# Polynomial attention in a six-layer perceiver: order of the turns on TensorE, and of two low halves on GpSimd

## The chip, the cores and the metric

The kernel runs on one core of one Trainium2 chip. The metric is the device time of one execution in microseconds. The times below are of three runs of the kernel before, and one further execution was profiled.

## The reference, cut to what matters

Six layers follow one another on x (32 sequences of 32 tokens, 512 wide): a cross attention, an attention, a low-rank mixture, a second cross attention, the polynomial attention, and a mixture of experts. The change touches the fifth layer only, which the kernel runs in one stage together with the end of the fourth layer (its output projection) and the beginning of the sixth (layer norm and router logits):

```python
q1, k1 = (proj(Wq1), proj(Wk1)); q2, k2 = (proj(Wq2), proj(Wk2)); v = proj(Wv)
q1, k1 = (_apply_rotary(q1, cos, sin), _apply_rotary(k1, cos, sin))
q2, k2 = (_apply_rotary(q2, cos, sin), _apply_rotary(k2, cos, sin))
s1 = jnp.einsum('bqhd,bkhd->bhqk', q1, k1)
s2 = jnp.einsum('bqhd,bkhd->bhqk', q2, k2)
pattern = jnp.where(causal[None, None], s1 / D * (s2 / D), 0.0)
y = jnp.einsum('bhqk,bkhd->bqhd', pattern, v).reshape(B, T, C)
return y @ Wout.T
```

## The kernel before

Every float32 operand of a product is held as two float16 halves, a high and a low one, and `product` (L102 to L108) issues three matmuls for each: high by high, high by low, low by high. ScalarE makes the high half of a value, and VectorE or GpSimd the low half (the value less its high half).

The stage is `poly` (L1894). Its 1024 tokens are eight tiles of 128 rows. The stage runs in eleven slots s = 0 to 10, and each slot works on up to four tiles, one in each step of a pipeline: t = s (output projection of the layer before, residual, norm), b = s - 1 (the four projections with their rotations and the values), q = s - 2 (scores, patterns, attention product) and r = s - 3 (output projection of the attention, residual, second norm, router logits). The order of the work within a slot is written out by hand, once for each engine, in the loops over SLOTS at L2001 (GpSimd), L2107 (VectorE), L2199 (ScalarE) and L2314 (TensorE). Engines wait for one another by semaphores with constant counts.

Terms of the change, with their functions:

- A turn (`turn`, L2251) is four 128x128 transposes on TensorE into the one bank `pl_bT`. Each turn first waits until the low half of the turn before has been taken out of that bank. `turn_mat(m, b)` turns the rotated matrix m of tile b, after which ScalarE (`mat_high`, L2171) and VectorE (`mat_low`, L2075) take the halves. `turn_norm("a", t, ya)` turns the normed rows of tile t, and `turned_high` (L2167) and `turned_low` (L2071) take the halves into `pl_LT`, which the next slot's projections read.
- `rotate(m, b)` (L1982, GpSimd) adds the two parts of rotated matrix m that VectorE's `rope` has written.
- `pattern_low(g, q)` (L1990, GpSimd) makes the low half of pattern g, after ScalarE's `pattern_high` (L2179).
- `attend(q)` (L2302, TensorE), the attention product, waits for all four low patterns and for the low half of the values (`value_low`, L2080), and writes `pl_bO`. `out_high` (L2185) and `out_low` (L2097) turn it into `pl_yT`, which the next slot's output projection reads first of all.

At the end of a slot TensorE does: project(3), turn_mat(1), values, turn_mat(2), attend, turn_norm, router logits. The next slot begins with the output projection, turn_mat(3) and project(0).

Of the kernel before, what the change touches and what calls it, by code (L numbers as in the profile page):

```python
# [1893 lines left out]
def poly(st):  # L1894
# [8 lines left out]
    with ExitStack() as c:  # L1903
# [8 lines left out]
        ya, ye = one("ya", [P, D]), one("ye", [P, D])  # L1912
# [44 lines left out]
        @block.gpsimd  # L1957
        def _(pool):
            pool.memset(mask[:, :], 1.0 / (HD1 * HD1)).then_inc(sig["p_const"], 1)
            pool.wait_ge(sig["p_const"], 1)  # L1960

            pool.affine_select(out=mask[:, :], in_=mask[:, :], compare_op=ALU.is_ge, fill=0.0, base=0,
                               pattern=[[1, P]], channel_multiplier=-1).then_inc(sig["p_const"], 1)
            pool.wait_ge(sig["p_const"], 2)

            m4 = mask[:, :].rearrange("p (b s) -> p b s", b=BPT)
            pool.affine_select(out=m4, in_=m4, compare_op=ALU.is_ge, fill=0.0, base=0,
                               pattern=[[-S, BPT], [0, S]], channel_multiplier=1).then_inc(sig["p_const"], 1)

            def bias_o(t):  # L1970
                pool.tensor_tensor(X[:, t, :], X[:, t, :], rows[:, :], ALU.add).then_inc(sig["p_xbo"], 1)

            def power(n, t):
                _, mv, rs = norms["ae".index(n)]
                pool.wait_ge(sig[f"p_{n}_var"], t + 1)
                if t:
                    pool.wait_ge(sig[f"p_{n}_y"], t)
                pool.tensor_tensor(rs[:, 0:1], mv[:, 2:3], mhalf[:, 0:1], ALU.pow).then_inc(sig[f"p_{n}_pow"], 1)
                pool.wait_ge(sig[f"p_{n}_pow"], t + 1)
                pool.tensor_scalar(rs[:, 1:2], rs[:, 0:1], mv[:, 0:1], -1.0, ALU.mult, ALU.mult).then_inc(sig[f"p_{n}_rstd"], 1)  # L1980

            def rotate(m, t):  # L1982
                pool.wait_ge(sig[f"p_rb{m}"], 2 * t + 2)
                if m >= 2:
                    pool.wait_ge(sig[f"p_mT{m - 2}"], t + 1)
                elif t:
                    pool.wait_ge(sig[f"p_mT{m + 2}"], t)
                pool.tensor_tensor(rr[m % 2][:, :], ra[m % 2][:, :], rb[m % 2][:, :], ALU.add).then_inc(sig[f"p_rr{m}"], 1)

            def pattern_low(g, t):  # L1990
                pool.wait_ge(sig[f"p_pathi{g}"], t + 1)
                ps = pat[:, :, g * BPT:(g + 1) * BPT, :]
                pool.tensor_tensor(ps[:, 1, :, :], pf[g % 2][:, :, :], ps[:, 0, :, :], ALU.subtract).then_inc(sig[f"p_patlo{g}"], 1)

            def rows_low(t):
                pool.wait_ge(sig["p_xrhi"], t + 1)
                pool.tensor_tensor(xr[t % 2][:, 1, :], ye[:, :], xr[t % 2][:, 0, :], ALU.subtract).then_inc(sig["p_xrlo"], 1)

            pool.wait_ge(sig["p_in"], 32)
            bias_o(0)  # L2000
            for s in range(SLOTS):  # L2001
                t, b, q, r = lanes(s)
                if r is not None:
                    power("e", r)
                if b is not None:
                    rotate(0, b)
                if q is not None:
                    pattern_low(0, q)
                if b is not None:
                    rotate(1, b)  # L2010
                if q is not None:
                    pattern_low(1, q)
                if t is not None:
                    power("a", t)
                    if t + 1 < NT:
                        bias_o(t + 1)
                if b is not None:
                    rotate(2, b)
                if r is not None:
                    rows_low(r)  # L2020
                if q is not None:
                    pattern_low(2, q)
                if b is not None:
                    rotate(3, b)
                if q is not None:
                    pattern_low(3, q)

        @block.vector
        def _(dve):
# [45 lines left out]
            def mat_low(m, t):  # L2075
                dve.wait_ge(sig[f"p_mhi{m}"], t + 1)
                to = mT[m][t % 2]
                dve.tensor_tensor(to[:, 1, :, :], quads(bT[:, :]), to[:, 0, :, :], ALU.subtract).then_inc(sig[f"p_mlo{m}"], 1)
# [28 lines left out]
            for s in range(SLOTS):  # L2107
                t, b, q, r = lanes(s)
                if r is not None:
                    residual_p(r)  # L2110
                if q is not None:
                    mat_low(3, q)
                if b is not None:
                    rope(0, b)
                if q is not None:
                    if q == 0:
                        dve.wait_ge(sig["p_const"], 3)
                    pattern(0, q)
                if b is not None:
                    rope(1, b)  # L2120
                if q is not None:
                    pattern(1, q)
                if t is not None:
                    residual_o(t)
                if s == 0:
                    for n in range(*MP):
                        split(n)
                if b is not None:
                    mat_low(0, b)
                    rope(2, b)  # L2130
                if q is not None:
                    pattern(2, q)
                if r is not None:
                    turned_low("e", r, XT[:, :, :, r * P:(r + 1) * P])
                if q is not None:
                    pattern(3, q)
                if b is not None:
                    rope(3, b)
                    mat_low(1, b)
                    value_low(b)  # L2140
                    mat_low(2, b)
                if q is not None:
                    out_low(q)
                if t is not None:
                    turned_low("a", t, LT)
                if s == 1:
                    for n in range(*UP):
                        split(n)
                if r is not None:
                    logits(r)  # L2150

        @block.scalar
        def _(act):
# [45 lines left out]
            for s in range(SLOTS):  # L2199
                t, b, q, r = lanes(s)  # L2200
                if q is not None:
                    mat_high(3, q)
                if r is not None:
                    scale("e", r, ye)
                    rows_high(r)
                if q is not None:
                    pattern_high(0, q)
                    pattern_high(1, q)
                if b is not None:
                    mat_high(0, b)  # L2210
                if s == 0:
                    split(MP[0])
                    split(MP[0] + 1)
                if t is not None:
                    scale("a", t, ya)
                if s == 0:
                    for n in range(MP[0] + 2, MP[1]):
                        split(n)
                if r is not None:
                    turned_high("e", r, XT[:, :, :, r * P:(r + 1) * P])  # L2220
                if q is not None:
                    pattern_high(2, q)
                if b is not None:
                    mat_high(1, b)
                if q is not None:
                    pattern_high(3, q)
                if b is not None:
                    value_high(b)
                    mat_high(2, b)
                if q is not None:  # L2230
                    out_high(q)
                if t is not None:
                    turned_high("a", t, LT)
                if s == 1:
                    for n in range(*UP):
                        split(n)

        @block.tensor
        def _(pe):
# [74 lines left out]
            for s in range(SLOTS):  # L2314
# [26 lines left out]
                if b is not None:  # L2341
                    project(3, b)
                    turn_mat(1, b)
                    values(b)
                    turn_mat(2, b)
                if q is not None:
                    wait_after("p_xo", min(s + 1, NT))
                    if r is not None:
                        pe.wait_ge(sig["p_xp"], r + 1)
                    attend(q)  # L2350
                if t is not None:
                    turn_norm("a", t, ya)
                if r is not None:
                    pe.wait_ge(sig["p_te_lo"], r + 1)
                    wait_after("p_pf3", min(r + 2, NT))
                    rows_times(bS[:, 0, 0:E1], lambda k: hl(XT, k, slice(r * P, (r + 1) * P)), Wr, E1).then_inc(sig["p_lg"], 1)


def experts(st):
# [453 lines left out]
```

## Time and profile before

| | us |
|---|---|
| median of three runs | 1955.49 |
| lowest, highest | 1949.67, 1959.02 |
| profiled execution, own time | 1950.19 |
| its span, first to last instruction | 1948.5 |
| TensorE (PE) busy in it | 1635.4 |
| VectorE (DVE) busy | 1301.4 |
| ScalarE (ACT) busy | 957.0 |
| GpSimd (POOL) busy | 616.8 |

The mean granted TensorE clock was 0.939 of full speed. Rows of a timeline give the start, the duration, the engine, the line of the kernel, the operation, what it writes and reads, its shape and how many equal ones are merged (x4); in brackets stands how long the engine had been idle before it, and whom the view names as the one that ended that. PE is TensorE's matmuls.

### The profile page before, as it was taken

To read this page: it belongs to the slowest core of one execution; us is meant where nothing else is said; L and a number is where in the kernel's file an instruction comes from. 1 tells how busy PE (TensorE), PEld (TensorE's weight loads), DVE (VectorE), ACT (ScalarE), POOL (GpSimd) and SP (SyncE) were. 2 spreads that over 40 slices of the span, in tenths; PEclk is the share of its full clock that TensorE was granted. 3 is DMA by queue.
4 is the path that set the end of the run, shared out by engine and by line. 5 is a ranking of instruction groups with operands and counts; after the bars stand their busy time and mean duration, and the time that the engine had idled before them with its cause. 6 is when DMAs were issued, how large, how long until landed. Compare 5 with 4: busy or idle time off the path is not lost. (4 is left out here: it accounts for less than half of the span.)

```text
span 1948.5 us, 43594 instructions
## 1 busy us (share of the span) xinstructions
PE 1635.4 (84%) x15542; PEld 1112.1 (57%) x15542; DVE 1301.4 (67%) x2926; ACT 957.0 (49%) x2169; POOL 616.8 (32%) x730
## 2 busy tenths in 40 slices
PE   6959999999976888399889889759996189989996
PEld 3525555555544666366666666525554077777775
DVE  7858888888855777367777777667775654454441
ACT  5635656565544344255565565533333255565551
POOL 4544545454522110111111111025544123333332
PEclk9989999999987999699999999979998589999998
DMA  5111101011130000101011001330000475665512
GB/s 192 50 49 31 41 30 41 30 41 30 33 124 12 1 2 2 56 27 33 25 32 33 26 31 33 133 133 29 12 12 12 152 223 146 164 186 157 143 31 67
DMA packets 50064, 126.86 MB, mean 65 GB/s; under 512 B 6913, under 2 KB 19425, under 8 KB 49889
## 3 DMA queue, kind: packets, MB, share of 16 engines
q1 hardware_dynamic: 44914, 113.10, 17.9%
q0 software_dynamic: 5008, 11.80, 3.1%
q8 instruction: 97, 1.59, 0.3%
q14 instruction: 45, 0.37, 0.1%
HBM read 111.29 MB, written 15.68 MB: 65 GB/s over the span
## 5 line engine op out<-in xcount | busy, mean ns | idle before, releaser
L106 PE MATMUL e_pGU<-XT,WB 128*128 128x128 f16 x1344 | 233.3, 222 | 18.9 <-issue 9.6
L107 PE MATMUL e_pGU<-XT,WB 128*128 128x128 f16 x1344 | 233.2, 222 | 0.0
L108 PE MATMUL e_pGU<-XT,WB 128*128 128x128 f16 x1344 | 233.2, 222 | 0.0
L2506 DVE SCALAR_TENSOR_TENSOR WB<-w5in,WB 128x1024 f16<-128x1024 f32 x96 | 115.5, 1223 | 85.9 <-ACT WB L2649 85.9
L1639 POOL TENSOR_TENSOR dLT<-dx,dLT 128x768 f16<-128x768 f32 x32 | 52.7, 1647 | 356.6 <-DVE dLT L1663 356.6
L106 PEld LDWEIGHTS e_pGU<-XT,WB 128*128 128x128 f16 x1344 | 134.0, 100 | 24.4 <-issue 22.8
L107 PEld LDWEIGHTS e_pGU<-XT,WB 128*128 128x128 f16 x1344 | 134.0, 100 | 1.5
L108 PEld LDWEIGHTS e_pGU<-XT,WB 128*128 128x128 f16 x1344 | 134.1, 100 | 0.0
L106 PE MATMUL dpK<-dLT,W 128*128 128x256 f16 x384 | 105.9, 276 | 19.0 <-POOL dLT L1639 19.0
L2489 POOL TENSOR_TENSOR XT<-e_mf,XT 128x256 f16<-128x256 f32 x84 | 56.2, 670 | 174.1 <-ACT XT L2663 174.1
L706 POOL TENSOR_TENSOR crn<-css,mhalf 128x8 f32<-128x8 f32 x64 | 106.6, 1666 | 5.3
L107 PE MATMUL dpK<-dLT,W 128*128 128x256 f16 x384 | 105.9, 276 | 0.0
L108 PE MATMUL dpK<-dLT,W 128*128 128x256 f16 x384 | 105.8, 276 | 0.0
L106 PE MATMUL dpV<-W,dLT 128*128 128x512 f16 x192 | 73.1, 381 | 38.0 <-DVE dvb L1675 38.0
L2649 ACT ACTIVATE WB<-w5in 128x1024 f16<-128x1024 f32 x96 | 97.9, 1044 | 13.6 <-PE e_pY L108 12.6
L106 PE MATMUL cpK<-W,cLT 128*128 128x512 f16 x192 | 73.9, 385 | 35.1 <-DVE ckh L757 30.9
L2623 DVE SCALAR_TENSOR_TENSOR e_mf<-e_pGU,e_sg 128x256 f32<-128x256 f32 x84 | 35.4, 421 | 84.8 <-ACT e_sg L2661 84.8
L1779 ACT ACTIVATE dpr<-dpS,dnm 128x257 f32<-128x257 f32 x128 | 59.0, 473 | 65.8 <-DVE dnm L1682 65.8
L131 POOL TENSOR_TENSOR rs<-mv,mhalf 128x1 f32<-128x1 f32 (+1 forms) x81 | 56.8, 701 | 90.6 <-DVE mv L126 90.6
L107 PE MATMUL cpK<-W,cLT 128*128 128x512 f16 x192 | 73.5, 383 | 0.0
L877 ACT ACTIVATE csq<-cpK 128x512 f32<-128x512 f32 x64 | 38.2, 597 | 71.7 <-PE cpK L108 71.0
L108 PE MATMUL cpK<-W,cLT 128*128 128x512 f16 x192 | 73.3, 382 | 0.0
(517 smaller groups left out, 5610.4 us busy)
## 6 DMA issues: line engine op xcount, KB each, us to landing
w5in<-in_WE SPq DMA_DIRECT2D x96, 512.0 KB, 4.7
cx<-in_ctx SPq DMA_DIRECT2D x32, 384.0 KB, 3.1
dx<-in_ctxT SPq DMA_DIRECT2D x32, 384.0 KB
w5in<-in_W SPq DMA_DIRECT2D x14, 512.0 KB, 8.6
wpiece<-in_W SPq DMA_DIRECT2D x12, 512.0 KB, 9.3
w3in<-in_W SPq DMA_DIRECT2D x11, 512.0 KB, 9.0
v<-vlat SPq DMA_DIRECT2D x32, 96.0 KB
X<-in_x SPq DMA_DIRECT2D x8, 256.0 KB, 8.2
```

The lines of the kernel that those rows point to most:

```text
L106: pe.matmul(out, lh, rh, start=first, stop=False, skip_group_check=shared)
L107: pe.matmul(out, lh, rl, start=False, stop=False, skip_group_check=shared)
L108: return pe.matmul(out, ll, rh, start=False, stop=last, skip_group_check=shared)
L131: pool.tensor_tensor(rs[0:rows, :], mv[0:rows, 2:3], half[0:rows, 0:1], ALU.pow).then_inc(self.rstd, 1)
L706: pool.tensor_tensor(rn[:, :], ss[:, :], mhalf[:, 0:H0], ALU.pow).then_inc(sig["c0_rn"], 1)
L877: act.activation(sq[:, :], pK[:, :], ACT.Square).then_inc(sig["c0_sq"], 1)
L1639: pool.tensor_tensor(LT[u][:, 1, :, :], xT[u][:, :, :], LT[u][:, 0, :, :], ALU.subtract).then_inc(sig["d_xlo"], 1)
L1779: act.activation(pr[:, g, :], pS[:, g, 0:SC], ACT.Exp, bias=nm[:, g:g + 1], scale=SCALE, accum_out=rsum[:, g:g + 1]).then_inc(sig["d_exp"], 1)
L2489: pool.tensor_tensor(mT[:, 1, 2 * g:2 * g + 2, :], mf[g % 2][:, :].rearrange("p (a n) -> p a n", a=2), mT[:, 0, 2 * g:2 * g + 2, :], ALU.s ...
L2506: dve.scalar_tensor_tensor(WB[w][:, 1, a], ring[n][:, :], WS, WB[w][:, 0, a], ALU.mult, ALU.subtract)\
L2623: dve.scalar_tensor_tensor(mf[g % 2][:, :], pGU[g % 2][:, 2 * T:4 * T], 1.0 / WS, sg[g % 2][:, :], ALU.mult, ALU.mult)\
L2649: act.activation(WB[w][:, 0, a], ring[n][:, :], ACT.Copy, scale=WS).then_inc(sig["e_whi"], 1)
```

## The change

On GpSimd the last low pattern of a slot comes before the last rotation. On TensorE the turn of the normed rows of tile t moves ahead of the attention product, and the turn of the third matrix of tile b moves behind the attention product and the router logits. ScalarE and VectorE take the halves in the new order.

```diff
@@ gpsimd
                     pattern_low(2, q)
+                if q is not None:
+                    pattern_low(3, q)
                 if b is not None:
                     rotate(3, b)
-                if q is not None:
-                    pattern_low(3, q)
@@ vector
                     value_low(b)
-                    mat_low(2, b)
-                if q is not None:
-                    out_low(q)
                 if t is not None:
                     turned_low("a", t, LT)
+                if q is not None:
+                    out_low(q)
+                if b is not None:
+                    mat_low(2, b)
@@ scalar
                     value_high(b)
-                    mat_high(2, b)
-                if q is not None:
-                    out_high(q)
                 if t is not None:
                     turned_high("a", t, LT)
+                if q is not None:
+                    out_high(q)
+                if b is not None:
+                    mat_high(2, b)
@@ tensor
                     values(b)
-                    turn_mat(2, b)
+                if t is not None:
+                    turn_norm("a", t, ya)
                 if q is not None:
                     wait_after("p_xo", min(s + 1, NT))
                     if r is not None:
                         pe.wait_ge(sig["p_xp"], r + 1)
                     attend(q)
-                if t is not None:
-                    turn_norm("a", t, ya)
                 if r is not None:
                     pe.wait_ge(sig["p_te_lo"], r + 1)
                     wait_after("p_pf3", min(r + 2, NT))
                     rows_times(bS[:, 0, 0:E1], lambda k: hl(XT, k, slice(r * P, (r + 1) * P)), Wr, E1).then_inc(sig["p_lg"], 1)
+                if b is not None:
+                    turn_mat(2, b)
```

## Rows read from the trace of the kernel before

**Rows 1.** The page: busy time of the engines, and the granted clock in 40 slices.
```profile
PE 1635.4 (84%) x15542; PEld 1112.1 (57%) x15542; DVE 1301.4 (67%) x2926; ACT 957.0 (49%) x2169; POOL 616.8 (32%) x730
...
PEclk9989999999987999699999999979998589999998
```
**Rows 2.** Windows, slots 4, 6, 8, 9: length; PE, PEld, DVE, ACT, POOL busy; clock; DMA.
```profile
1359.94:1385.78 25.84, 24.10 (x265) 13.29 (x265) 18.95 (x38) 9.19 (x15) 13.60 (x14) 1.00 0.03 11
...
1411.70:1439.20 27.50, 25.76 (x265) 13.71 (x265) 18.96 (x38) 9.19 (x15) 13.59 (x14) 0.93 0.03 12
...
1466.69:1491.45 24.76, 21.37 (x249) 11.51 (x249) 17.24 (x34) 7.97 (x13) 11.54 (x11) 1.00 0.03 12
1491.45:1511.15 19.70, 8.93 (x176) 6.21 (x177) 9.11 (x17) 5.64 (x9) 6.54 (x7) 0.64 0.04 15
```
**Rows 3.** Waits of PE in slots 3 to 7: us in total, times, longest.
```profile
PE pl_bO L106 <- DVE pl_v L2083: 6.0, 5, 1.3
PE pl_bO L106 <- DVE pl_yT L2099: 3.8, 6, 0.9
```
**Rows 4.** Timeline of PE from the end of slot 4 into slot 5.
```profile
1381.69 0.60 PE L2255 MATMUL pl_bT<-ident,pl_rr 128*128 128x128 f32 x4
1383.46 0.27 PE L106 MATMUL pl_bO<-pl_pat,pl_v 128*32 128x128 f16 x4 [1.17 <-DVE pl_v L2083]
...
1384.27 0.66 PE L2255 MATMUL pl_bT<-ident,pl_ya 128*128 128x128 f32 x4
1384.76 0.17 PE L106 MATMUL pl_bS<-W,XT 128*128 128x8 f16 x1
...
1385.78 0.39 PE L106 MATMUL pl_bO<-W,pl_yT 128*128 128x512 f16 x1 [0.57 <-DVE pl_yT L2099]
...
1388.38 0.60 PE L2255 MATMUL pl_bT<-ident,pl_rr 128*128 128x128 f32 x4
```
**Rows 5.** Timeline of GpSimd, end of slot 4.
```profile
1378.66 1.16 POOL L1993 TENSOR_TENSOR pl_pat<-pl_pf,pl_pat 128x512 f16<-128x512 f32 x1
1380.82 1.27 POOL L1988 TENSOR_TENSOR pl_rr<-pl_ra,pl_rb 128x512 f32<-128x512 f32 x1 [1.00 <-DVE pl_rb L2069]
1382.05 1.16 POOL L1993 TENSOR_TENSOR pl_pat<-pl_pf,pl_pat 128x512 f16<-128x512 f32 x1
```
**Rows 6.** Timeline of VectorE, end of slot 4.
```profile
1380.66 0.68 DVE L2078 TENSOR_TENSOR pl_mT<-pl_bT,pl_mT 128x512 f16<-128x512 f32 x1
1382.52 0.69 DVE L2083 SCALAR_TENSOR_TENSOR pl_v<-pl_bM,pl_v 128x512 f16<-128x512 f32 x1 [1.18 <-ACT pl_v L2177]
1383.13 0.68 DVE L2078 TENSOR_TENSOR pl_mT<-pl_bT,pl_mT 128x512 f16<-128x512 f32 x1
1385.03 0.69 DVE L2099 TENSOR_TENSOR pl_yT<-pl_bO,pl_yT 128x512 f16<-128x512 f32 x1 [1.22 <-ACT pl_yT L2189]
```
**Rows 7.** Timeline of ScalarE, end of slot 4.
```profile
1379.79 0.62 ACT L2183 ACTIVATE pl_pat<-pl_pf 128x512 f16<-128x512 f32 x1
...
1384.40 0.60 ACT L2189 ACTIVATE pl_yT<-pl_bO 128x512 f16<-128x512 f32 x1 [1.43 <-PE pl_bO L108]
```
**Rows 8.** Timelines of GpSimd, VectorE and PE at the attention product of slot 2.
```profile
1330.32 1.15 POOL L1993 TENSOR_TENSOR pl_pat<-pl_pf,pl_pat 128x512 f16<-128x512 f32 x1
...
1330.90 0.69 DVE L2083 SCALAR_TENSOR_TENSOR pl_v<-pl_bM,pl_v 128x512 f16<-128x512 f32 x1 [1.29 <-ACT pl_v L2177]
...
1331.72 0.25 PE L106 MATMUL pl_bO<-pl_pat,pl_v 128*32 128x128 f16 x3 [1.04 <-DVE pl_v L2083]
```
**Rows 9.** Timelines of GpSimd, VectorE and PE at the attention product of slot 8.
```profile
1487.63 1.16 POOL L1993 TENSOR_TENSOR pl_pat<-pl_pf,pl_pat 128x512 f16<-128x512 f32 x1
...
1487.78 0.69 DVE L2083 SCALAR_TENSOR_TENSOR pl_v<-pl_bM,pl_v 128x512 f16<-128x512 f32 x1 [0.85 <-ACT pl_v L2177]
...
1489.13 0.26 PE L106 MATMUL pl_bO<-pl_pat,pl_v 128*32 128x128 f16 x4 [1.43 <-POOL pl_pat L1993]
```
**Rows 10.** Timeline of PE at the output projection that begins slot 6.
```profile
1412.10 0.63 PE L107 MATMUL pl_bO<-W,pl_yT 128*128 128x512 f16 x1
```

More of the change, by code:

```diff
@@ L2140, in _ @@
                     value_low(b)
-                    mat_low(2, b)
+                if t is not None:
+                    turned_low("a", t, LT)
                 if q is not None:
                     out_low(q)
-                if t is not None:
-                    turned_low("a", t, LT)
+                if b is not None:
+                    mat_low(2, b)
                 if s == 1:
@@ L2228, in _ @@
                     value_high(b)
-                    mat_high(2, b)
+                if t is not None:
+                    turned_high("a", t, LT)
                 if q is not None:
                     out_high(q)
-                if t is not None:
-                    turned_high("a", t, LT)
+                if b is not None:
+                    mat_high(2, b)
                 if s == 1:
@@ L2344, in _ @@
                     values(b)
-                    turn_mat(2, b)
+                if t is not None:
+                    turn_norm("a", t, ya)
                 if q is not None:
@@ L2350, in _ @@
                     attend(q)
-                if t is not None:
-                    turn_norm("a", t, ya)
                 if r is not None:
```

## The prediction

> **What bounds the kernel now.** I read the page first. TensorE (PE) is busy for 84% of the span and its granted clock is at or near full speed in most slices [rows 1], so the question is only what PE waits for in the stretch that the edit touches. The polynomial attention stage runs from about 1262 to 1525 us, in eleven slots (0 to 10). I cut it by slots in the windows view, from the first matmul of one output projection to the first of the next [rows 2]. Slot 4 takes 25.84 us with PE busy for 24.10. Slots 3 to 7 are alike except that 6 takes 27.50 at a mean clock of 0.93, and 7 the same (two such rows, of which the first stands). The ends are looser: slot 8 has PE busy for 21.37 of 24.76 us, slot 9 for 8.93 of 19.70. So PE bounds the steady slots, and reordering can only recover its idle time.
>
> Then the waits of PE over slots 3 to 7 [rows 3]. There are two kinds only: 6.0 us before the attention product (five times) and 3.8 us before the output projection (six times, since the window catches one more boundary). The timeline of PE in slot 4 shows both [rows 4]: the turn of the third matrix at 1381.69, idle 1.17 us, the attention product at 1383.46, the turn of the normed rows at 1384.27, the eight-column logits product at 1384.76, idle 0.57 us, and the output projection at 1385.78. Everything that this edit can win in a steady slot lies in those 1.74 us.
>
> **Who ends the wait before the attention product.** It waits for four low patterns from GpSimd and for the low half of the values from VectorE. The view of waits names VectorE. But in slot 4 pattern_low(3) runs on GpSimd from 1382.05 for 1.16 us, to 1383.21 [rows 5], and value_low on VectorE from 1382.52 for 0.69, also to 1383.21 [rows 6]. A tie, so the name proves nothing. I compare slots. In slots 3 to 7 the product starts 0.25, 0.25, 0.35, 0.25 and 0.35 us after GpSimd's end, and as long after VectorE's. Slot 2 parts them: GpSimd ends at 1331.47, VectorE at 1331.59, and the product starts at 1331.72, which is 0.25 after the one and 0.13 after the other [rows 8]. In slot 8 GpSimd ends at 1488.79, VectorE at 1488.47, and the product starts at 1489.13 [rows 9]. A release from VectorE is elsewhere quick: the output projection at 1385.78 starts 0.06 us after out_low's end at 1385.72 [rows 4, 6]. So I take GpSimd as the true last releaser in slots 3 to 8, with a delay of 0.25 to 0.35.
>
> **Part 1: pattern_low(3) ahead of rotate(3) on GpSimd.** Nothing is added; two instructions change places. In slot 4 pattern_low(2) ends at 1379.82 and ScalarE's high pattern 3 at 1379.79 + 0.62 = 1380.41 [rows 5, 7]. So pattern_low(3) can run from about 1380.45 to 1381.6 in place of 1382.05 to 1383.21. The product then waits for VectorE's value_low alone, at 1383.21. With a VectorE release of 0.06 to 0.13 us it starts at 1383.27 to 1383.34, not 1383.46. Over slots 3 to 7 the delay now is 0.25, 0.25, 0.35, 0.25 and 0.35, sum 1.45 us; less 5 x 0.06 to 0.13 that leaves 0.80 to 1.15, and I take 0.95. Slot 2 gives 0 to 0.07; I take 0. In slot 8 the product now starts 1489.13 - 1488.47 = 0.66 us after value_low [rows 9]; less 0.06 to 0.13 that gives 0.53 to 0.60, say 0.55. Slot 9 has no rotation, so nothing changes there. Sum: **1.5 us**. If the view of waits is right instead and VectorE needs those 0.25 to 0.35 itself, slots 2 to 7 give nothing and slot 8 gives 0.66 - 0.35 = 0.3. So part 1 lies between -0.3 and -1.8 us.
>
> The price is rotate(3), which starts at 1381.6 instead of 1380.82 and ends near 1382.9. Its reader, turn_mat(3) in the next slot, comes at 1388.38 [rows 4], with 5.5 us to spare, and the next GpSimd work waits for a residual after the output projection, which starts only at 1385.78. Cost nothing. If that cover were gone, it would be at most the 0.8 us of delay per slot.
>
> **Part 2: the turn of the normed rows ahead of the attention product, the third matrix's turn behind it and behind the logits.** No work is added. The two turns are equal on PE: about 0.60 and 0.66 us in the rows [rows 4]. What fills the time before the attention product is still one turn, and what fills the time before the output projection is still one turn and the logits. The chain that ends each idle stretch isn't touched: values on PE, value_high on ScalarE, value_low on VectorE for the first; out_high at 1384.40 and out_low at 1385.03 for the second [rows 6, 7]. On both engines what now stands ahead is of the same kind and length (turned_high for mat_high, turned_low for mat_low). So the steady slots gain 0 from it, within 0.05 us a slot from the issue order. I follow each new wait:
> The turn of the normed rows needs the turning bank free, that is mat_low(1), at 1380.66 + 0.68 = 1381.34 [rows 6]; PE comes at 1381.69. Its rows were scaled by ScalarE several us before.
> The third matrix's turn now needs turned_low, which takes mat_low(2)'s old place behind value_low and ends near 1383.8. PE comes near 1384.4. No wait.
> mat_high(2) and mat_low(2) now stand behind out_high and out_low. The turn runs 1384.4 to 1385.05, the high half to 1385.7, the low half to 1386.4. turn_mat(3), which needs the bank, comes at 1388.38 less what part 1 saves: 2 us to spare. Queued behind mat_low(2) on VectorE are the logits copy and residual_p; the latter waits for the output projection's end at 1388.4 anyway.
> Slot 1 has three turns in a row, each waiting for the one before. The order of the two changes and the sum does not: 0. Slot 8 has no normed rows, so the turn leaves the time before the attention product and its idle stretch grows by as much, while the idle stretch ahead of the output projection, which stays bound by out_low, shrinks: 0.
> Sum of part 2: 0, between -0.5 and +0.5 us.
>
> **The clock** is the larger unknown. In this trace slots 6 and 7 begin their output projection at the lower level of 1.2 GHz, seen in matmuls of 0.63 us, against 0.38 to 0.39 in slot 5 [rows 4, 10]. That costs each slot 27.50 - 25.84 = 1.66 us; slots 3, 4, 5 and 8 begin at 2.4 GHz [rows 2]. What precedes is the same loose stretch in all: idle 1.17, a short product, a turn, the logits, idle 0.57. The change shortens that by 0.2 us and keeps its make-up, so I expect about the same number of falls: 0, with +/-1.66 for each fall more or fewer. The Trainium skill, TensorE: Matmul & The Clock Gate, section A second HAM failure mode: psum-queue depth-cycling, says that small idles between groups of matmuls can make the clock oscillate. The trace agrees in two of six slots; by that rule every such boundary could fall, which is rival A.
>
> **Rivals.**
> A, slower: the clock falls at all six boundaries of slots 3 to 8 instead of two. Four more falls at 1.66 are 6.6; less 1.5 this gives +5.1 us against before, 1960.6. It decides from the first fall more on, as that alone outweighs part 1. For it: the stretch of weak activity stays and two of six fell already. Against: it gets shorter. Chance 0.08.
> B, faster by more: the falls of slots 6 and 7 go, 3.3 us, with part 1 in all 4.8: 1950.7. Chance 0.08.
> C, the change doesn't do what it says: VectorE was the releaser, the waits stay and only slot 8 gives 0.3: 1955.2. For it: the name in the waits; against: slots 2 and 8. Chance 0.14.
> D, slower: the third matrix's low half comes late for turn_mat(3). It has 2 us of cover; if the whole ScalarE and VectorE chain slipped by 3 us, 1 us in each of six slots would be +6 - 1.5 = +4.5, 1960.0. Nothing in the rows slips so far. Chance 0.02.
>
> **How the numbers follow.** The profiled execution took 1950.19 us (span 1948.5), the lowest of the runs shown being 1949.67 and the highest 1959.02, median 1955.49. Against the profiled one the forecast is 1950.2 - 1.5 = 1948.7; carried over to the median, 1955.5 - 1.5 = **1954.0 us**, chance 0.68. The spread of the runs themselves (9.4 us) is wider than all the bounds above. I take the low end as the lowest run less 1.8, so 1947.9, rounded to 1947.5, and the high end as rival A, 1960.5; this leaves 2 in 10 out at most. 0.5% is 9.8 us, about what a measurement of this kernel can tell from no change. No case above reaches it alone; only scatter of the runs does: faster 0.03, same 0.95, slower 0.02.
>
> **What would show it right or wrong.** In the changed profile pattern_low(3) on GpSimd should end 1.6 us before value_low in the steady slots, the idle before the attention product should be 0.1 to 0.2 us shorter, and that before the output projection still 0.5 to 0.6. Slot 4 should take about 25.65 us, slot 8 about 24.2. turn_mat(3) should follow the output projection without idle. If the idle before the attention product is as long as before, C holds; count the output projections that start with matmuls of 0.63 us for A and B. The prediction is wrong if a steady slot at full clock is longer than 25.9 us or shorter than 25.3.

## The result

Fifteen runs of each kernel: before 1951.6 us in the median (1946.37 to 1959.48), after 1939.21 (1935.68 to 1944.05). The ratio is 0.9933, 95% interval 0.992 to 0.9946: 0.67% faster, where 1954.0 us and no measurable change were forecast. The profiled execution of the changed kernel took 1936.71 us (span 1935.0). A later measurement of the two gave 0.9944 (0.993 to 0.9958).

The page after, to be held against [rows 1]: TensorE is busy for the same share, and the engines' totals hardly move.

```profile
PE 1631.3 (84%) x15542; PEld 1108.5 (57%) x15542; DVE 1302.1 (67%) x2926; ACT 958.1 (50%) x2169; POOL 617.8 (32%) x730
...
PEclk9979999999997999699999999969998599999998
```

The windows of slots 4, 6, 8 and 9 after (columns as in [rows 2]), each again from one output projection to the next:

```profile
1356.71:1381.32 24.61, 24.14 (x265) 13.22 (x265) 19.03 (x37) 9.23 (x15) 13.62 (x14) 1.00 0.04 12
...
1405.93:1430.54 24.61, 24.14 (x265) 13.23 (x265) 19.04 (x37) 9.23 (x15) 13.61 (x14) 1.00 0.03 12
...
1455.15:1478.00 22.85, 21.27 (x249) 11.42 (x249) 16.74 (x32) 8.51 (x14) 11.56 (x11) 1.00 0.04 14
1478.00:1497.33 19.33, 8.52 (x177) 5.89 (x177) 9.87 (x18) 5.72 (x10) 6.55 (x7) 0.71 0.04 15
```

Slot 4 fell from 25.84 to 24.61 us with the same work on PE: 1.23 us of idle time is gone. Slot 6 fell from 27.50 to 24.61: the same 1.23, and 1.66 because it no longer begins at 1.2 GHz. The gains by slot are 0.94 up to the end of slot 2, then 1.21, 1.23, 1.31, 2.89, 2.88, 1.91 (slot 8) and 0.37 (slot 9); slot 10 is 1.10 longer, at a lower clock. In all 11.6 us, from the first matmul of the stage to the start of the next stage (256.81 to 245.17 us). Of it 3.3 is clock won in slots 6 and 7 and 1.1 is clock lost in slot 10. The other 9.4 us are waits but for two small parts that vary without any change of order: slot 9, which took 19.35 to 19.70 us in three traces with the old order (its 0.37), and slot 0, which was 0.17 longer after. The gain of slot 2 by itself is 1.11 us: from the turn ahead of its attention product to the next output projection it took 4.06 us before and 2.95 after. The two spans differ by 13.5; the remaining 1.9 us lie in other stages, whose time differs by 7.4 us between two traces of the changed kernel.

The waits of PE in slots 3 to 7 after, in place of the two of [rows 3]:

```profile
PE pl_bT L2257 <- DVE pl_LT L2073: 2.4, 5, 0.5
```

And the end of slot 4 in the timeline of PE, then of GpSimd, then of VectorE, against [rows 4], [rows 5] and [rows 6]:

```profile
1378.46 0.60 PE L2257 MATMUL pl_bT<-ident,pl_ya 128*128 128x128 f32 x4
1378.99 0.26 PE L106 MATMUL pl_bO<-pl_pat,pl_v 128*32 128x128 f16 x4
...
1379.79 0.18 PE L106 MATMUL pl_bS<-W,XT 128*128 128x8 f16 x1
...
1380.72 0.63 PE L2257 MATMUL pl_bT<-ident,pl_rr 128*128 128x128 f32 x4 [0.47 <-DVE pl_LT L2073]
1381.32 0.39 PE L106 MATMUL pl_bO<-W,pl_yT 128*128 128x512 f16 x1
```

```profile
1377.26 1.16 POOL L1993 TENSOR_TENSOR pl_pat<-pl_pf,pl_pat 128x512 f16<-128x512 f32 x1 [0.66 <-ACT pl_pat L2184]
1378.38 1.27 POOL L1988 TENSOR_TENSOR pl_rr<-pl_ra,pl_rb 128x512 f32<-128x512 f32 x1
```

```profile
1379.29 0.69 DVE L2083 SCALAR_TENSOR_TENSOR pl_v<-pl_bM,pl_v 128x512 f16<-128x512 f32 x1 [1.18 <-ACT pl_v L2178]
1379.90 0.68 DVE L2073 TENSOR_TENSOR pl_LT<-pl_bT,pl_LT 128x512 f16<-128x512 f32 x1
1380.57 0.69 DVE L2099 TENSOR_TENSOR pl_yT<-pl_bO,pl_yT 128x512 f16<-128x512 f32 x1
```

The attention product starts at 1378.99, as soon as the turn before it is through. VectorE's value_low, which was to hold it until its end, only starts at 1379.29. So the product does not wait for this value_low at all. The code says why: attend(q) waits for p_vlo to reach q + 1, and value_low(b) of the same slot belongs to tile b = q + 1 and raises it to q + 2. The low half that the product reads was made a whole slot earlier. Nor does the product wait for pattern_low(3) any more: it starts 0.57 us after its end (1377.26 + 1.16 = 1378.42), more than the 0.25 to 0.35 that the release took before.

The idle time of 1.17 us is gone, and 0.47 us are left before the third matrix's turn, which now waits for turned_low. The output projection starts at 1381.32, 0.06 after out_low ends (1380.57 + 0.69 = 1381.26), and 2.33 us after the start of the attention product, against 1385.78 - 1383.46 = 2.32 before. So it is still as late as the chain over out_high and out_low makes it, and the turn, which is through at the same time, now fills that time.

### The profile page after: what moved, and what is told of

The parts are those of the page before. It is cut to its first block and busy times, and to the rows that moved or that the text cites. A ratio compares the mean times of both kernels' runs of the same rounds, so it can differ in the third digit from the quotient of the medians.

```text
span 1935.0 us, 43594 instructions
## 1 busy us (share of the span) xinstructions
PE 1631.3 (84%) x15542; PEld 1108.5 (57%) x15542; DVE 1302.1 (67%) x2926; ACT 958.1 (50%) x2169; POOL 617.8 (32%) x730
## 5 line engine op out<-in xcount | busy, mean ns | idle before, releaser
L106 PE MATMUL cpK<-W,cLT 128*128 128x512 f16 x192 | 74.4, 388 | 34.0 <-DVE ckh L757 29.9
```

Of the source, the lines that this page charges most:

```text
L106: pe.matmul(out, lh, rh, start=first, stop=False, skip_group_check=shared)
```

## The experiments

**Which of the two edits makes the gain.** First the edit on GpSimd alone, in the kernel before:

```diff
                     pattern_low(2, q)
+                if q is not None:
+                    pattern_low(3, q)
                 if b is not None:
                     rotate(3, b)
-                if q is not None:
-                    pattern_low(3, q)
```

> The kernel before with one edit: on GpSimd pattern_low(3) comes ahead of rotate(3). TensorE, ScalarE and VectorE keep their old order. Theory now: the attention product waits for the low patterns alone, since the low half of the values that it reads was made in the slot before; then this edit alone removes the whole 1.17 us before it, and a steady slot at full clock falls from 25.84 to about 24.6 to 24.8 us, in all 8 to 12 us, ratio 0.994 to 0.996. Rival 1, the new order on TensorE makes the gain: this kernel then equals the one before within 2 us, slot 25.7 to 25.85. Rival 2, the prediction's: VectorE's value_low is next to end the wait and the product starts no earlier than its end: slot 25.65.

Measured: 1941.35 us against 1952.41, ratio 0.9941 (0.9927 to 0.9955). Steady slots take 24.77 us. The waits of PE in slots 3 to 7:

```profile
PE pl_bT L2255 <- DVE pl_mT L2078: 4.3, 5, 0.9
```

and the one at the end of slot 4 in its timeline:

```profile
1378.91 0.63 PE L2255 MATMUL pl_bT<-ident,pl_ya 128*128 128x128 f32 x4 [0.86 <-DVE pl_mT L2078]
```

There is no wait before the attention product any more. The next wait is 0.86 us long, for the low half that empties the turning bank. So GpSimd's edit alone brings 25.84 - 24.77 = 1.07 of the 1.23 us in a steady slot. Slot 2 gains 1.10 by it (4.06 to 2.96 us over the same stretch as above) and slot 8 gains 1.50 (24.76 to 23.26 us).

Then the new order of turns alone, the changed kernel with GpSimd's old order:

```diff
-                if q is not None:
-                    pattern_low(3, q)
                 if b is not None:
                     rotate(3, b)
+                if q is not None:
+                    pattern_low(3, q)
```

> The changed kernel with GpSimd's old order: rotate(3) ahead of pattern_low(3). TensorE, ScalarE and VectorE have the new order of turns. Theory now: the wait for the last low pattern stands where it stood, idle 1.1 to 1.2 us before the attention product, slot 25.8 us at full clock, ratio 0.999 to 1.001. Rival 1, the order of turns makes the gain: slot 24.6, ratio 0.993 to 0.995.

Measured: 1951.66 against 1952.41 us, ratio 1.0 (0.9988 to 1.0012); steady slots 25.83. The waits of PE in its slots 3 to 7 are of the same two kinds and lengths as in the kernel before:

```profile
PE pl_bO L106 <- DVE pl_v L2083: 5.8, 5, 1.2
PE pl_bO L106 <- DVE pl_yT L2099: 3.2, 5, 0.9
```

The order of turns is worth nothing by itself, as forecast. On top of the early pattern it is worth 24.77 - 24.61 = 0.16 us a slot: the logits now stand ahead of the last turn and fill part of the wait for the bank (0.86 to 0.47 us). Slot 2 has no logits, and there the order is worth nothing (2.96 against 2.95). In slot 8 it is worth 23.26 - 22.85 = 0.4 for another reason: there are no normed rows to turn, so the product no longer stands behind a turn and starts 0.39 us earlier in the slot (20.53 after its begin, against 20.92). These 1.2 us are too little for the measured times to show (0.9941 against 0.9933).

**Does the product wait for value_low.** One edit of the kernel before, on VectorE:

```diff
                     mat_low(1, b)
-                    value_low(b)
-                    mat_low(2, b)
+                    mat_low(2, b)
+                    value_low(b)
```

> The kernel before with one edit: on VectorE value_low(b) comes behind mat_low(2, b), so that it ends about 0.6 us later in each slot (1383.8 in place of 1383.2 on the clock of the profile before). Theory now: the attention product does not wait for it in this slot and starts as before, before value_low has ended; idle before it 1.17 us, slot 25.84. Rival 2, the prediction's: VectorE's value_low is the next to end that wait and the product starts behind it, 0.4 to 0.6 us later, slot 26.3.

Measured: 1950.03 against 1952.41 us, ratio 0.9994 (0.9979 to 1.0009), steady slots 25.82 to 25.83. The wait of PE before the product in slots 3 to 7:

```profile
PE pl_bO L106 <- POOL pl_pat L1993: 5.8, 5, 1.2
```

and the timelines of PE and VectorE at the end of slot 4:

```profile
1383.04 0.27 PE L106 MATMUL pl_bO<-pl_pat,pl_v 128*32 128x128 f16 x4 [1.16 <-POOL pl_pat L1993]
...
1383.20 0.68 DVE L2083 SCALAR_TENSOR_TENSOR pl_v<-pl_bM,pl_v 128x512 f16<-128x512 f32 x1
```

The product starts at 1383.04 and value_low at 1383.20. The idle time is unchanged, and since value_low has moved out of the way the same view now names GpSimd: the product starts 0.25 us after the low pattern's end (1382.78) and 0.84 before value_low's (1383.88). This and the trace after settle the releaser: GpSimd alone.

**How much room the early pattern has.** The changed kernel, with two spare sums before the last pattern:

```diff
                 if q is not None:
+                    pool.tensor_tensor(spare[:, :], rows[:, :], rows[:, :], ALU.add).then_inc(sig["p_spare"], 1)
+                    pool.tensor_tensor(spare2[:, :], rows[:, :], rows[:, :], ALU.add).then_inc(sig["p_spare"], 1)
                     pattern_low(3, q)
```

> The changed kernel with two spare sums of 128x512 on GpSimd (about 1.25 us each, into tiles that nobody reads) ahead of pattern_low(3). GpSimd idles 0.66 us there in the changed kernel, so the last low pattern ends about 1.85 us later. Theory now: the attention product starts 0.25 to 0.35 us behind it, 1.5 to 1.6 later than in the changed kernel; the slot grows by as much, to 26.1 to 26.2 us at full clock, and the loose stretch at the end of the slot is back, so that one to four of the six output projections of slots 3 to 8 start at 1.2 GHz again, 1.7 us each. In all 10 to 17 us slower than the changed kernel, ratio to the one before 0.999 to 1.003. Rival, the clock falls have nothing to do with that stretch: none of the six starts at 1.2 GHz, ratio 0.999 or less.

Measured: 1947.17 against 1952.41 us, ratio 0.9972 (0.996 to 0.9984), steady slots 25.56. GpSimd at the end of slot 4:

```profile
1375.45 1.04 POOL L2025 TENSOR_TENSOR pl_spare<-pl_rows 128x512 f32<-128x512 f32 x1
1376.44 1.04 POOL L2026 TENSOR_TENSOR pl_spare<-pl_rows 128x512 f32<-128x512 f32 x1
1377.44 1.15 POOL L1994 TENSOR_TENSOR pl_pat<-pl_pf,pl_pat 128x512 f16<-128x512 f32 x1
```

The expected slot of 26.1 to 26.2 us was too long, and for two reasons that fit the mechanism. The sums take 0.99 us from start to start, not 1.25, so the pattern is 2 x 0.99 - 0.66 = 1.32 us later. And in the changed kernel it had room: it ended at 1378.42, its release takes 0.25, and the product came at 1378.99, 0.32 later. That leaves 1.0; measured are 25.56 - 24.61 = 0.95 us a slot. The clock part of the expectation failed outright: none of the seven output projections of slots 3 to 9 began at 1.2 GHz. The loose end of the slot was only partly back, with 0.89 us idle before the product instead of 1.17.

**The clock.** I counted the output projections of slots 3 to 9 that begin at 1.2 GHz in each trace. The kernel before and the changed one were traced again:

> The kernel before, once more, to count the output projections of slots 3 to 9 that start at 1.2 GHz (in the first trace two of seven). Theory: one or two of seven, each 1.7 us; full-clock slots 25.84. Rival, that the first trace was an exception: none.

> The changed kernel, once more, for the same count (in its first trace none of seven). Theory: none, slots 3 to 7 24.6 us each. Rival: as many as in the kernel before, one or two.

The kernel before (1950.71 us) had two of seven again. This is the one of slot 6, at half the rate of the 0.39 us ones:

```profile
1410.90 0.61 PE L106 MATMUL pl_bO<-W,pl_yT 128*128 128x512 f16 x1 [0.57 <-DVE pl_yT L2099]
```

The changed one (1939.91 us) had none, and slots of 24.60 to 24.61 us. A third trace of it, timed with others:

> The changed kernel, on the same chip as the filled one and the one before, to compare the three. Theory: ratio to the one before 0.992 to 0.995, steady slots 24.6, none of the output projections of slots 3 to 9 at 1.2 GHz. Rival: one or two of them at 1.2 GHz.

Measured: 1941.5 against 1952.23 us, ratio 0.9944 (0.993 to 0.9958), none of seven. For the other side the spare sums were made four. A first version gave each a tile of its own and did not fit on the chip (the next tile needed 2048 B a partition, 1088 B were left); so the second pair goes into the same two tiles, behind a wait for the first:

> As the run with two spare sums on GpSimd ahead of pattern_low(3), but with four; each took 1.04 us there, 0.99 from start to start. The attention product is about 2 us later again: idle before it 2.9 us, slot 25.56 + 1.98 = 27.5 us where the clock stays at 2.4 GHz. Theory of the clock: the looser the end of the slot, the more of the seven output projections of slots 3 to 9 start at 1.2 GHz; four to seven here, 1.7 us each, so the kernel takes about 1966 to 1976 us. Rival: the falls are independent of it, zero to two of seven, about 1961 to 1965 us.

Measured: 1974.56 us, ratio 1.0116 (1.0099 to 1.0134). The product's idle time was 3.01 us (2.9 expected), and all seven output projections began at 1.2 GHz. The windows of slots 5 and 6:

```profile
1392.04:1421.95 29.91, 26.77 (x264) 14.32 (x265) 19.04 (x37) 8.71 (x16) 17.58 (x18) 0.90 0.03 10
1421.95:1449.98 28.03, 24.46 (x265) 13.28 (x265) 19.04 (x37) 9.74 (x16) 17.59 (x18) 0.99 0.03 11
```

Slots alternate between long ones (29.7 to 29.9 us) and short ones (27.9 to 28.0), against an estimated 27.5 at full clock (25.56 + 1.98). In the short ones the clock had already fallen by the attention product of the slot before, and only one or two matmuls of the output projection still ran at 1.2 GHz. All traces together, by the idle time at the end of each slot:

| idle before the attention product | traces, slots | next output projection at 1.2 GHz |
|---|---|---|
| 4.82 us and more | all twelve traces, slot 9 | 12 of 12 |
| 3.01 to 3.77 us | four spare sums, slots 2 to 8 | 7 of 7 |
| 1.42 to 1.92 us | before (twice), value_low late, two spare sums, turns alone, slot 8 | 0, 0, 0, 0, 1 of 1 each |
| 1.04 to 1.31 us | before (twice), value_low late, turns alone, slots 2 to 7 | 2, 2, 1, 0 of 6 each |
| 0.89 to 1.01 us | two spare sums, slots 2 to 7 | 0 of 6 |
| at most 0.27 us | after (three times), GpSimd alone, and the two filled kernels below, slots 2 to 8 | 0 of 42 |

The one fall of the kernel with the turns alone came behind the longest idle of its row, 1.92 us. The count goes with the idle time: all above 3 us, some between 1 and 2, none where the product hardly waits. So the changed kernel's none is no accident of one trace. What follows the product differs too (the idle of 0.57 us before the output projection is gone with the other), and these runs don't part the two. Slot 9 has other long waits besides. The Trainium skill (TensorE: Matmul & The Clock Gate, A second HAM failure mode: psum-queue depth-cycling) says that small idles between groups of matmuls, where they are frequent enough, make the clock oscillate. The traces agree for idles of 1.04 to 1.92 us, 6 of 29 of which were followed by a fall, and show none below. Where the falls set in stays open, as 0 of 6 at 0.89 to 1.01 us and 5 of 24 at 1.04 to 1.31 us are too few to tell apart.

**Can the rest be filled.** The remaining 0.47 us is a wait for the bank between two turns with only 1 us of work between them. In a further version project(0) of the next slot comes behind the logits, and the turns of the normed rows and of matrix 1 stand on either side of values (TensorE's part of the edit, cut to the end of the slot):

```diff
                     project(3, b)
-                    turn_mat(1, b)
-                    values(b)
                 if t is not None:
                     turn_norm("a", t, ya)
+                if b is not None:
+                    values(b)
+                    turn_mat(1, b)
...
+                if t is not None:
+                    project(0, t)
                 if b is not None:
                     turn_mat(2, b)
```

> The changed kernel, with the remaining idle of a steady slot (0.47 us before the third matrix's turn) filled: project(0, t) of the next slot comes behind the router logits, ahead of turn_mat(2, b); turn_norm(a) comes ahead of values and turn_mat(1) behind it, into a doubled pl_LT; project(1) ahead of scores(0); VectorE and ScalarE follow, and pl_t1 is single to make room. Theory: once the last low pattern is early, the end of the slot is a chain of turns through one bank, and with 2.6 us of projection between two turns no wait is left; steady slot 24.61 to about 24.0 to 24.2 us, 2 to 4 us less in all than the changed kernel, ratio to the one before 0.990 to 0.993. Rival: a step that is now later (scores(0), the low half of matrix 0, the last rotation) turns into the next wait; slot 24.6 us or more and idle before a product of scores or a turn.

Measured: 1944.22 against 1951.69 us, ratio 0.9963 (0.995 to 0.9975), where 0.990 to 0.993 was expected and the changed kernel had 0.9933. The steady slots did come down to 24.20 to 24.21 us, but one wait appeared in the filling of the pipeline: slot 3 began 73.16 us after the stage's first matmul, against 64.89 in the changed kernel. PE's waits from 1300 to 1335:

```profile
PE pl_bT L2259 <- DVE pl_mT L2078: 6.1, 1, 6.1
PE pl_bM L106 <- DVE pl_v L2083: 1.1, 1, 1.1
```

and VectorE's timeline there:

```profile
1313.69 2.46 DVE L2033 SCALAR_TENSOR_TENSOR W<-w5in,W 128x1024 f16<-128x1024 f32 x3 [4.35 <-ACT W L2160]
```

Three weight pieces stood in VectorE's queue ahead of mat_low(2, 0), which this version has at the start of the next slot, and VectorE itself waited 4.35 us for their high halves from ScalarE. VectorE's part of them is moved behind it:

```diff
-                if s == 1:
-                    for n in range(*UP):
-                        split(n)
...
                     mat_low(2, q)
+                if s == 2:
+                    for n in range(*UP):
+                        split(n)
```

> As the run with the slot's end filled, but VectorE's low halves of the last three weight pieces come in slot 2 behind mat_low(2, 0), no longer at the end of slot 1 ahead of it. Theory: the 6.08 us idle of TensorE before the third matrix's turn at the end of slot 1, which that run had, was those 2.5 us of VectorE and the weight pieces' ScalarE halves ahead of mat_low(2, 0); it goes down to under 1.5 us, steady slots stay 24.2, and the kernel is 4 to 8 us faster than that run and 1 to 4 us faster than the changed kernel, ratio to the one before 0.991 to 0.9935. Rival: the weights only wait elsewhere, idle of over 2 us in slot 2 or before the output projection of slot 3, no faster than the changed kernel.

Measured: 1936.14 against 1952.23 us, ratio 0.9925 (0.9912 to 0.9938), next to the changed kernel's 0.9944 on the same chip. The same wait is now a little above the 1.5 us expected:

```profile
PE pl_bT L2259 <- DVE pl_mT L2078: 1.7, 1, 1.7
```

and the window of a steady slot (columns as in [rows 2], this time from one project(1) to the next):

```profile
1354.10:1378.30 24.20, 24.16 (x280) 13.04 (x271) 18.77 (x38) 9.28 (x16) 13.50 (x15) 1.00 0.12 44
```

PE is busy for 24.16 of 24.20 us: by order no more than 0.04 us is left to win in a steady slot. The stage took 242.47 us, 2.6 less than the changed kernel's 245.06 in that job. The intervals of the two ratios still overlap, so that it is faster than the changed kernel is shown for one trace of each and only made likely by the times.

## Why the prediction was wrong

**What held.** PE bounds the steady slots and the change can only recover its idle time. GpSimd is the last releaser, 0.25 to 0.35 us ahead of the product. pattern_low(3) moved as worked out (it ends 1.56 us before value_low, where the two had ended together), and rotate(3) and the third matrix's turn cost nothing: turn_mat(3) follows the output projection without idle in every slot. The new order of turns alone is worth 0. So rival D never came up.

**The step that failed** is in part 1: "The product then waits for VectorE's value_low alone, at 1383.21". This put a floor under the gain which isn't there. The name in the view of waits [rows 3] and a tie of two ends at 1383.21 [rows 5, 6] made value_low the next to end the wait. The waiting instruction asks for a count, and that count had been reached a slot earlier. Without that floor, the working of the prediction itself would have given the product right behind the turn: 1.17 us a slot, and then some of it back in the wait for the bank. The term was 0.95 us over slots 3 to 7 and measured, with GpSimd's edit alone, 5 x 1.07 = 5.4 at full clock; for slot 2 it was 0 and measured 1.10; for slot 8 it was 0.55 and measured 1.50. In place of the 1.5 us of part 1 that makes 8.0. The sign of being wrong that the prediction named, a steady slot at full clock shorter than 25.3 us, came with 24.61. Both bounds of part 1 (-0.3 and -1.8 us) shared the error, as both took value_low for a condition; so did rival C. The trace before held no row that could show this, as value_low ended before the product in every slot; the code did, in the count that attend(q) asks of p_vlo.

**Part 2** was given 0. That is right without the early pattern. With it, the bank became the next wait, and the new order is worth 0.16 us in each of slots 3 to 7 and 0.4 in slot 8, about 1.2 us in all. The prediction didn't ask what is late next after a gain of the full 1.17 us.

**The clock** was given 0, "about the same number of falls". Rival B, with a chance of 0.08, had it: the falls of slots 6 and 7 went, 3.3 us in the trace. Its size of 4.8 us in all was too small, because its other part, the 1.5 us of part 1, was. The 1.1 us that slot 10 lost at the lower clock had no term. The changed kernel's slot 10 took about 15.06 us in all three of its traces, but so it did with value_low late, where the order there is the old one (13.96 in the trace before), so no run shows the loss to come from the change.

**The range** ended at 1947.5, the lowest run less 1.8. The text itself named 1.74 us a slot as all there was to win; six slots of that, with 3.3 us of clock, is some 14 us and would have reached 1942. Part of the miss of 14.8 us isn't the change's: the median of fifteen runs of the kernel before is 1951.6, 3.9 us under that of the first three. The gain itself is 12.4 us, against 1.5 forecast.

## What to carry to other kernels

Before a wait is put down to an instruction, compare the count that the waiting engine asks for with the iteration that raises it. In a pipeline written over several slots, the instruction nearest in time can serve the next tile. When two candidates end at the same time, a bound for the gain has to include the case that one of them isn't a condition at all. And when the last releaser is moved up, follow the chain to the next thing that is truly late, here a single bank with turns too close together.

## What the runs showed of the hardware

Idle stretches of TensorE of 1.04 to 1.31 us before the attention product, with 0.56 to 0.95 us more before the next projection, went with a start of that projection at 1.2 GHz in 5 of 24 cases, ones of 3.01 to 3.77 us in 7 of 7, and ones of 0.27 us or less in 0 of 42. In the two traces of the kernel before and the one with value_low late, each such start made its slot 1.5 to 1.7 us longer. In the trace after, clock made 3.3 - 1.1 = 2.2 of the stage's 11.6 us. From the end of a GpSimd instruction of about 1.16 us, as the profile gives it, to the start of the matmul that waited for it, 0.25 to 0.35 us passed, against 0.05 to 0.15 from the end of a VectorE instruction (0.06 for the output projection, 0.15 for a turn).
